# A graph transformer on one core: the gather of the edges' records moved behind the last q, k, v product

## The reference

```python
xn = _layernorm(x, axis=-1)
x = x + _L0_gnn_ref(xn, src, dst, ...) + _L0_mix_ref(xn[None], ...)[0]
...
def _L0_gnn_ref(node_feats, src, dst, ...):
    neigh = jax.ops.segment_sum(node_feats[src], dst, num_segments=n)
    ...
def _L0_mix_ref(x, ...):
    xn = rmsnorm(x, g_pre)
    q, k, v = jnp.split(xn @ w_qkv, 3, axis=-1)
    ...
    q = jax.nn.softmax(q, axis=-2) * SCALE
    k = jax.nn.softmax(k, axis=-1)
    context = jnp.einsum('bhdn,bhen->bhde', k, v)
    out = jnp.einsum('bhde,bhdn->bhen', context, q)
```

## Time and profile before

| | |
|---|---|
| time of the profiled execution | 2221.48 us |
| its span on the core | 2220.0 us |
| mean granted clock of TensorE | 0.978 |
| busy, share of the span | PE 94%, DVE 75%, ACT 56%, POOL 27% |
| runs shown, median | 2213.01 us |

### The profile page before, as it was taken

The page is one execution under the profiler, slowest core; times in us unless marked ns, Lnnn a source line. Parts: engine busy times, 40 slices in busy tenths (PEclk is TensorE's granted clock), DMA queues, the critical chain, the costliest instruction groups (busy, mean ns, idle before and its releaser), DMA issues. The chain is left out here.

```text
span 2220.0 us, 46547 instructions
## 1 busy us (share of the span) xinstructions
PE 2078.1 (94%) x17896; PEld 1947.2 (88%) x17896; DVE 1656.2 (75%) x3107; ACT 1232.8 (56%) x2876; POOL 594.2 (27%) x462
## 2 busy tenths in 40 slices
PE   5659999999879999998999999999999999999997
PEld 3549999999779999997788999999989999999996
DVE  6898888886588888885667666565567868888885
ACT  5656555554537767765543444444444336767664
POOL 3100000000037777771000000000000015767774
PEclk9879999999989999999999999999999999999998
DMA  4424343334448777875003666466641026777876
GB/s 122 148 62 119 95 117 91 114 98 131 161 156 229 229 234 223 242 213 135 1 26 107 188 188 189 115 182 194 188 142 42 25 94 193 233 231 220 245 217 169
DMA packets 241111, 339.00 MB, mean 153 GB/s; under 512 B 33407, under 2 KB 202546, under 8 KB 240754
## 3 DMA queue, kind: packets, MB, share of 16 engines
q1 hardware_dynamic: 208908, 296.19, 42.6%
q0 software_dynamic: 28528, 35.76, 8.6%
q10 hardware_dynamic: 3446, 3.97, 0.6%
HBM read 258.89 MB, written 76.95 MB: 151 GB/s over the span
## 5 line engine op out<-in xcount | busy, mean ns | idle before, releaser
L2457 PE MATMUL bank<-WB_r,XN_r 128*128 128x448 f32 x1400 | 398.7, 366 | 0.4 <-DVE X L2250 0.4
L2008 POOL DMA_INDIRECT SC<-xd,slot_i x128 | 185.6, 1450 | 792.9 <-DVE slot_q L1644 662.2
L2411 DVE TENSOR_TENSOR WB_r<-WB,WB_r 128x448 fp32r<-128x448 f32 x350 | 218.0, 634 | 165.6 <-ACT WB_r L2406 165.6
L2406 ACT CAST WB_r<-WB 128x448 fp32r<-128x448 f32 x350 | 198.2, 568 | 244.9 <-PE bank L2457 242.5
L2457 PEld LDWEIGHTS bank<-WB_r,XN_r 128*128 128x128 f32 x1400 | 262.5, 188 | 23.0 <-DVE X L2250 0.8
L1938 PE MATMUL bank<-SC_r,WB_r 128*128 128x256 f32 (+1 forms) x2064 | 250.7, 280 | 8.6 <-issue 6.2
L1938 PEld LDWEIGHTS bank<-SC_r,WB_r 128*128 128x128 f32 x2064 | 244.1, 188 | 13.0 <-issue 12.8
L1058 ACT CAST WB_r<-bank 128x200 fp32r<-128x200 f32 x391 | 145.0, 371 | 159.3 <-PE bank L1041 158.7
L1953 PE MATMUL bank<-R_r,H_r 128*128 128x256 f32 x1752 | 216.2, 283 | 4.7 <-DVE R_r L1849 4.7
L1953 PEld LDWEIGHTS bank<-R_r,H_r 128*128 128x128 f32 x1752 | 210.0, 190 | 5.1 <-issue 5.1
L2398 POOL TENSOR_TENSOR WB<-WB,CB 128x128 f32<-128x128 f32 (+1 forms) x56 | 28.4, 512 | 592.6 <-DMA WB<-adjw 591.7
(11 more groups left out here) (460 smaller groups left out, 5134.1 us busy)
## 6 DMA issues: line engine op xcount, KB each, us to landing
WB<-adjw SPq DMA_DIRECT2D x350, 224.0 KB, 2.8
WB<-in_f_pack SPq DMA_DIRECT2D x127, 512.0 KB
WB<-in_f_pack SPq DMA_DIRECT2D x62, 640.0 KB
adjw<-X SPq DMA_DIRECT2D x24, 1600.0 KB, 7.9
WB<-in_f_pack SPq DMA_DIRECT2D x65, 516.0 KB
xd<-XN SPq DMA_DIRECT2D x15, 640.0 KB, 5.5
y<-X SPq DMA_DIRECT2D x10, 640.0 KB, 3.3
X<-y SPq DMA_DIRECT2D x6, 640.0 KB, 7.0
```

What stands on the lines that cost most here:

```text
L2008: e.indirect_dma_start(yin[i % 2][:, q * D:(q + 1) * D], None, XD, bass.IndirectOffsetOnAxis(ap=slot_i[:, 2 * i + q:2 * i + q + 1], axis=0 ...
L2406: e.copy(split_w(m)[0], RAW[m % PR]).then_inc(S("whigh"), 1)
L2411: e.tensor_tensor(al, RAW[m % PR], ah.bitcast(F32), ALU.subtract).then_inc(S("wlow"), 1)
L2457: mm_ = e.matmul(conv_bank(k, band, c)[:, 0:PW], x[st][:, o], y, start=(st == 0 and i == 0), stop=(st == T - 1 and i == 2))
```

## The change

GpSimd waits for all 25 products (`qk`) before it gathers the edges' records. VectorE's `places_dve` moves from the front of the attention to behind k less its maximum, and `q_norm_dve(0)` now stands ahead of `inside_dve`. ScalarE's `places_act` moves behind the last exponential of k. The semaphores' values are numbered anew for this order. SyncE waits for `edges`, beside `qk`, before it stores the normalised rows.

```diff
@@ windows_dve @@
-        e.wait_ge(S("mix0_act"), M0A_PLACES)
+        e.wait_ge(S("mix0_act"), M0A_KEXP)
@@ windows_pool @@
         e.wait_ge(S("rows"), 2)
+        e.wait_ge(S("qk"), T)
         for g in range(WG):
             e.indirect_dma_start(h_all[:, 384 * g:384 * (g + 1)].bitcast(I32), None, a["edges"].rearrange("(r k) -> r k", k=3),
                                  bass.IndirectOffsetOnAxis(ap=beg4i[:, g:g + 1], axis=0)).then_inc(S("edges"), 16)
@@ program @@
-    M0A_PLACES, M0A_KEXP, M0A_MEM = WG - COUNTED, WG - COUNTED + 1, WG - COUNTED + 5
-    M0V_W, M0V_RS, M0V_GROW, M0V_REL, M0V_KMAX, M0V_DIAG, M0V_KSUB, M0V_MEM, M0V_MASKED, M0V_CTX, M0V_CWO = (
-        0, 2, 5, 6, 7, 8, 9, 13, 14, 15, 16)
+    M0A_KEXP, M0A_MEM, M0A_PLACES = WG - COUNTED, WG - COUNTED + 4, WG - COUNTED + 5
+    M0V_W, M0V_RS, M0V_GROW, M0V_KMAX, M0V_DIAG, M0V_KSUB, M0V_MEM, M0V_REL, M0V_MASKED, M0V_CTX, M0V_CWO = (
+        0, 2, 5, 6, 7, 8, 12, 13, 14, 15, 16)
@@ mix0_act @@
         q_exp_act(e, 0)
-        places_act(e)
         q_exp_act(e, 1)
...
         e.activation(memkT[:, :], memkT[:, :], ACT.Exp).then_inc(S("mix0_act"), 1)
+        places_act(e)
         x_sum_act(e, range(8, T))
@@ mix0_dve @@
-        places_dve(e, c)
         q_sub_dve(e, c, 1)
...
         e.tensor_tensor(memkT[:, :], memkT[:, :], kb[0:4, :], ALU.subtract).then_inc(S("mix0_dve"), 1)
+        places_dve(e, c)
+        q_norm_dve(e, c, 0)
         inside_dve(e)
-        q_norm_dve(e, c, 0)
         places_in_tiles_dve(e, c)
@@ sp_program @@
         e.wait_ge(S("qk"), T)
+        e.wait_ge(S("edges"), 16 * WG)
         store_sp(e, XD, XN, "xd_out", xn_ready(e, 0))
```

## The result

| | before | changed |
|---|---|---|
| median (4 runs each) | 2213.98 us | 2227.39 us |
| range of the runs | 2210.8 to 2216.18 | 2225.78 to 2228.52 |
| profiled execution, time / span | 2221.48 / 2220.0 | 2227.73 / 2226.2 |

The ratio is 1.0066, with a 95% interval of 1.0054 to 1.0077: 13.4 us slower. The forecast was slower by 7.7, 2220.7. Sign and range hold the result; the size was missed. The profiled execution of the changed kernel is the first of its four runs; the one of before is none of its four, and lies 5.3 us above the slowest of them.

The account below looks back on a forecast made before the run. VectorE bounds up to some 170 us, TensorE from 180. Last product 68.7, then gather, port, release, places, norm, inside count, sum and context, clock put the reciprocal at 106.3 against 98.64: +7.7, 2220.7 us; range 2214.8 to 2228.

Parts of the forecast that it names:

- the first term: Last product: without the edges' gather beside TensorE's products, they end at 68.7 instead of 74.95, 6.2 us earlier.
- I carry the difference over: The profiled execution's 8.5 us above the median was kept as an offset, turning 2229.2 into 2220.7.
- the stands are the program's, not the gather's: Rival: ScalarE and VectorE idle again at 57 to 65, gather starts at 75.2; +13.9 us, 2226.9; chance 0.16.
- signs by which I said that I would be wrong: Last product still at 75, VectorE not standing for the edges, or such stands behind 89 on the path.
- The transmission: Behind the context's reciprocal, VectorE keeps its order and distances, so its +7.7 us passes to the whole execution.
- The gather: GpSimd's edges: 17.9 us from first issue to last packet, plus 2.0 for the port and 0.1 release.
- The port's price: GpSimd's issues slowed beside VectorE's two-input operations in k's maximum and subtraction: 2 us, between 0 and 5.7.
- The clock: TensorE, cold after standing until 97.8, runs the context's products at half rate for a while: 1.5 us lost.
- The reciprocal: The context's reciprocal on VectorE starts at 106.3 instead of 98.64, 7.7 us later.
- the port's full block: Rival: GpSimd loses all the time of VectorE's two-input operations, 5.7 us instead of 2; +11.4, 2224.4; chance 0.08.
- the clock's absence: Rival "little lost": the port costs nothing and the clock little; 2 and 1.5 go, +4.2, 2217.2; chance 0.22.
- faster: Rival: edges in by 76.8, needing thirteen issues at 0.6 us each; 2208 at half the issue time; chance 0.05.

Follow-up runs that it names:

- b5: The kernel before, no edit, run again and profiled beside a5: 2212.48 us; last product ends at 67.2, reciprocal starts at 90.55.
- set 5: The last follow-up set, holding only the kernel before (2211.84 us) and the changed kernel (2225.51 us); ratio 1.0055.
- a5: The changed kernel, no further edit, run again beside b5: 2225.51 us, ratio 1.0055 to the kernel before.
- sets 2 to 4: Three follow-up sets with both kernels: before 2223.46, 2224.03, 2222.40 us; changed 2230.77, 2232.61, 2229.65 us.
- sets 1 to 4: Four follow-up sets, each running the kernel before beside variants: before 2222.82, 2223.46, 2224.03, 2222.40 us.
- b1: The kernel before, no edit, run again for a second profile: 2224.03 us, ratio 1.0002 to the kernel before in its set.
- b4: The kernel before, no edit, run again and profiled beside a4: 2222.44 us.
- order_early: The changed kernel without its two waits (GpSimd's for all products, SyncE's for the edges), keeping the new order: 2229.15 us, ratio 1.0027 to before.
- b2: The kernel before, no edit, run again for a third profile: 2223.05 us.
- mid14_total: mid17_total with GpSimd's wait at 14 products instead of 17: 2217.47 us, ratio 0.9978 to the kernel before.
- mid17: The changed kernel with GpSimd's wait at 17 products instead of 25 and nothing else: 2222.03 us, ratio 0.9999 to the kernel before.
- mid17_total: The changed kernel with GpSimd's wait at 17 products, and the inside counts' sum behind the context's products: 2216.36 us, ratio 0.9966 to before.
- a4: The changed kernel, no further edit, run again beside b4: 2229.65 us, ratio 1.0032 to the kernel before.
- warm62: The changed kernel with 62 instead of 24 TensorE warming products ahead of the inside sum: 2229.44 us, 3.2 less than a3.
- a3: The changed kernel, no further edit, run again: 2232.61 us, ratio 1.0036 to the kernel before in its set.
- swap_back: The changed kernel with the inside count ahead of the norm of q again: 2232.53 us, against 2230.77 for the changed kernel in its set.

## Why the prediction was right or wrong

**The step that failed** is the first term with what stood ahead of it: "I take these stands for the gather's doing. That is what the change can win back", 6.2 us, and at the end "that execution is 8.5 us above the median of the runs, 2213.01, so I carry the difference over". The 8.5 us were not a constant of the profiler. They were the stands: b5, in a set like the one that was timed, ends the last product at 67.2 where the profile of before has 74.95, and starts the reciprocal 8.1 us earlier, of 9.7 us between the two executions; the other 1.6 lie behind it and are not explained. The profile showed an execution of one kind, the median came from the other (the four timed runs of before left no profile of their own, so set 5 speaks for them), and in that kind the gather costs the products next to nothing: a5 ends them 1.35 us ahead of b5. In sets with stands the forecast of +7.7 stands beside +7.3, +8.6 and +7.2; where there are none the won 6.2 go to 1.35, which makes +12.6. In the profiles of set 5 the reciprocal moves by 14.8 and the execution by 13.7: the new chain behind the last product is 1.9 us longer than reckoned (most of it the clock), and 1.1 us is made up behind. That +7.7 came so close in sets 2 to 4 is in part luck, as the chain's errors below go both ways. My rival "the stands are the program's, not the gather's" came to +13.9 and to 2226.9, the right number by another way: there the stands would have stayed in both kernels; in set 5's two profiles, and in the changed kernel's of the timed set, there are none. None of the signs by which I said that I would be wrong turned up: the last product moved, VectorE stood for the edges, and no stand fell on the path behind 89. They all tested the changed kernel, and the fault lay in what it was measured from.

**Whether the gather makes the stands** is now half answered. All five profiles of the early gather in sets 1 to 4 (b1 to b4 and order_early) have them between 55 and 66, and none of the eight profiles of the same sets with the gather behind all products has one there: in such sets they go with the gather. But b5 gathers as early and has none. So they need the gather and something that the set brings; what that is stays open. It is not slower transfers: from the first issue to the last packet there are 18.3 us in b4 and 19.4 in b5. In b2 the first stand begins 8.5 us after the gather's first issue, and in mid14_total, whose gather starts at 53.9, 8.7 us after, as its expectation had it; mid17 and mid17_total, which start at 58.4 and 59.2, have none.

**The rest, point by point.**

The transmission held: in the changed kernel's first profile VectorE starts the count's first one-hot operation 5.8 us later than in the earlier trace rows's (145.31 against 139.50), for a reciprocal 5.9 us later, and the span is 6.2 longer. Over all twenty profiles the execution's time less the start of the reciprocal lies between 2119.8 and 2125.9, while the reciprocal itself moves by 19.7, from 90.55 to 110.28. It passes on, give or take 3 us.

The gather: from the first issue to VectorE's places I had 20.0 us; it is 19.0 in the changed kernel's profile and 20.4 in a5. The port's price was 0.56 us in the one and 1.7 in the other, against the 2 I took. The timeline of the changed kernel has VectorE's pair, each of 1.62 us:

```profile
73.96 3.16 DVE L921 TENSOR_TENSOR wide_wb<-wide_wb,small 128x1408 f32<-128x1408 f32 x2
```

and that of a5:

```profile
72.81 3.16 DVE L921 TENSOR_TENSOR wide_wb<-wide_wb,small 128x1408 f32<-128x1408 f32 x2
72.90 2.35 POOL L302 DMA_INDIRECT H<-in_edges,small  x1 [0.30 <-issue]
...
75.56 1.23 POOL L302 DMA_INDIRECT H<-in_edges,small  x1 [0.30 <-issue]
```

The Trainium skill's rule in "SBUF — State Buffer", section "SBUF: two separate sides" (full blocking by two-input operations), agrees with this trace in its mechanism. An issue that began 0.41 us before the end of such an operation took 0.28 more, one that began 1.53 before it (a5) took 1.40 more, and mid14_total and mid17 have 0.56, 0.82, 0.90 and 1.07 more for 0.69, 0.95, 1.03 and 1.20: each time what was left of the operation, less 0.13. An issue that began 0.04 us ahead of the pair (73.92) took its usual 0.95, and VectorE's operations take 1.62 beside the gather or not. What was wrong is the sum of 5.7 us, which had GpSimd lose all the time of all these operations: it loses only when an issue begins inside one, for the rest of that one. So 0.56 or 1.7 is a matter of where the issues fall, which the change does not set.

VectorE's wait: 8.83 us, "some 9" (10.2 and 10.4 in a4 and a5, which have the issue of 2.35 us). Places, norm and inside count: 6.56 us from the places' start to the inside count's, against 6.7. Both held in the changed kernel's first profile.

The clock: 2.5 to 3.0 us (warm62), against 1.5. The levels were right, 0.50 and 1.00 in the windows, but it stayed at the lower one for longer than after the shorter stands in the earlier trace rows: the stand was 14.9 us, and the products were 0.50 until 99 and at 0.80 in the mean of 99 to 103.

The reciprocal: 104.5 to 107.3 in five profiles of the changed kernel, forecast 106.3. The place of the new chain was right to 2 us; what it was measured from was not. In the first of these profiles that is errors that partly cancel: the last product 1.8 us earlier than reckoned (66.9), as the stand until 38.30 was missing there too, the gather 1.0 shorter, its start 0.5 later, the sum and the context 0.8 longer.

SyncE: at nothing, right. Its last late weight goes at 109.3 and the next store at 131.3.

The rivals: the port's full block is there, but not at its 5.7 us; the clock's absence is refuted by the rows above; faster was never near.

## What to carry to other kernels

When the profiled execution lies several us off the median of the timed runs, find out what in it makes the difference before any part of it is entered as a gain; a stall whose end names nothing is the first suspect, and a second profile of the same kernel is the cheapest experiment. A transfer moved behind a stage has to be laid against the first instruction that needs its data: here the best start of those tried was not "early" nor "behind the products" but 8 or 11 tiles sooner, so that the data land about when k's subtraction ends (mid17_total, 7.7 us faster than before where there are stands; mid14_total, 4.9). And a sum that only a later engine needs must not stand ahead of a chain that could run: it held 26 products back, on a TensorE whose clock fell meanwhile.

mid17_total was not run in a set without stands. Its reciprocal started at 93.17 in a profile that still had a stand of 5.54 us beside the gather of the destinations; before, without stands, reaches 90.55. Between a3 and a5 the last product moves by 2.6 us; taken off, that gives 90.6. So where there are no stands I estimate it level with the kernel before.

## What the runs showed that I had not expected

TensorE, too, stands for nothing that the profile names while GpSimd gathers. In warm62 it has only products that wait for no one, and yet, as its timeline shows:

```profile
81.68 0.59 PE L568 MATMUL bank<-CB 128*128 128x128 f32 x3 [0.32 <-issue]
83.09 0.62 PE L568 MATMUL bank<-CB 128*128 128x128 f32 x4 [0.82 <-issue]
85.22 1.10 PE L568 MATMUL bank<-CB 128*128 128x128 f32 x4 [1.51 <-issue]
87.35 9.27 PE L568 MATMUL bank<-CB 128*128 128x128 f32 x65 [1.03 <-issue]
```

These products read constants and write one bank. The stands end at 87.35, as the gather's last data have come (VectorE's places start at 88.13). With ScalarE and VectorE beside the early gather that makes three engines, each late in going on although what they waited for was there. Late semaphores would fit ScalarE and VectorE, but not TensorE, whose warming products wait for none. Late instructions would fit all three. The Trainium skill, "Runtime: NRT & Kernel Launch", section "Instruction fetch mechanics", has each sequencer fetch by a DMA queue of its own and calls the cost mostly hidden. The profile's DMA view has packets of the kind "instruction", on two queues, and they do not bear the second reading out. In the kernel before, its queues from 53.6 to 85.8, across the stands of 57 to 66:

```profile
q1 hardware_dynamic: 3358, 3.36, 31.6%
q0 software_dynamic: 581, 1.78, 20.1%
```

There is no instruction packet among them, and none between 32 and 39, beside the stand of 5.52 us. In warm62, from 81 to 88:

```profile
q0 software_dynamic: 321, 0.98, 50.5%
q8 instruction: 1, 0.02, 0.9%
```

One packet moved there, and TensorE stood four times, after every three or four products. Whether the view has the fetches of every engine is not shown. What holds the three engines stays open.

The order's clock cost in order_early (2.0 us) and in swap_back (1.1 us won and lost again) were the other surprise: moving work of another engine by 2 us can cost as much again in TensorE's clock.
